# A decoder layer on one core: low parts of the feed-forward weights on GpSimd, and head and last group in a new order

## The reference, cut to what matters

```
x = layernorm(x + gelu(x @ ((w1 @ w2^T) * sparse_mask) + b2))              # x: 4 x 256 x 512
q = x @ wq (32 heads of 128); k, v = ctx @ wk, ctx @ wv (8 groups); rope on q and k
x = layernorm(x + softmax(q k^T / sqrt(128) + mask) v @ wo)                # ctx: 4 x 64 x 512
base = x @ W^T + b
lora = sum over 8 experts of routing[b, e] * (x @ A[e]^T) @ B[e]^T * 2
routing = softmax(mean(x[:, 107:-1]) @ router_W^T + router_b)
out = layernorm(x + base + lora)
```

## Time and profile before

| | |
|---|---|
| median of 3 runs | 487.48 us (487.14 to 487.7) |
| the profiled execution's own time | 488.16 us |
| its span, first to last instruction | 486.4 us |
| TensorE busy | 471.9 us (97%) |
| VectorE busy | 403.4 us (83%) |
| ScalarE busy | 266.2 us (55%) |
| GpSimd busy | 253.8 us (52%) |
| mean granted TensorE clock | 0.990 of full speed |

### The profile page before, as it was taken

How to read it: one execution, slowest core, us unless ns; L and a number is a source line. 1 busy time by engine, 2 the same in 40 slices (tenths; PEclk the granted TensorE clock), 3 DMA queues, 4 the chain that set the end, 5 groups by cost and what they waited for, 6 DMA issues and landing times.

```text
span 486.4 us, 11234 instructions
## 1 busy us (share of the span) xinstructions
PE 471.9 (97%) x4293; PEld 393.0 (81%) x4293; DVE 403.4 (83%) x720; ACT 266.2 (55%) x460; POOL 253.8 (52%) x250
## 2 busy tenths in 40 slices
PE   8999999999999999999999999999999999789994
PEld 7878878887888888888888888888888888568873
DVE  2679988788888887888888888888887999987566
ACT  4573656835483648355644755384637444544434
POOL 3378536954494559356835774486539423022300
PEclk9999999999999999999999999999999999979998
DMA  8945100230023002301320230022002400000004
GB/s 269 355 157 175 44 1 1 89 130 3 1 86 129 0 0 92 123 0 27 112 77 0 84 110 22 0 86 86 0 0 88 67 1 2 1 0 1 0 2 173
DMA packets 29137, 31.56 MB, mean 65 GB/s; under 512 B 6321, under 2 KB 16817, under 8 KB 29114
## 3 DMA queue, kind: packets, MB, share of 16 engines
q1 hardware_dynamic: 29114, 31.25, 20.0%
HBM read 29.15 MB, written 2.10 MB: 64 GB/s over the span
## 4 chain that ended last, share of the span: by engine, by line
PE 94%; DVE 3%; ACT 2%; issue 1%; POOL 0%; POOLq 0%; ACTq 0%; DVEq 0%
PE bank L272 28%; PE bank L274 27%; PE bank L273 27%; PE bank L380 7%; PE bank L278 2%; PE bank L389 2%; DVE VWl L1166 1%; PE bank L293 1%; ACT VWh L813 1%; PE bank L286 0%; DVE QR L1200 0%; PE bank L414 0%; PE bank L447 0%; PE bank L333 0%; DVE X L1425 0%
## 5 line engine op out<-in xcount | busy, mean ns | idle before, releaser
L1760 POOL TENSOR_TENSOR QS<-QS,SIN 128x512 f32<-128x512 f32 x64 | 82.8, 1294 | 118.0 <-ACT QS L813 117.5
L1166 DVE TENSOR_TENSOR VWl<-bank,VWh 64x512 fp32r<-64x512 f32 x128 | 88.0, 687 | 16.0 <-ACT VWh L813 14.4
L272 PE MATMUL bank<-XTh,WQh 128*128 128x512 f32 x256 | 101.0, 395 | 0.0
L274 PE MATMUL bank<-XTh,WQl 128*128 128x512 f32 x256 | 99.8, 390 | 0.0
L273 PE MATMUL bank<-XTl,WQh 128*128 128x512 f32 x256 | 99.8, 390 | 0.0
L813 ACT ACTIVATE VWh<-bank 64x512 fp32r<-64x512 f32 x128 | 76.0, 594 | 29.3 <-PE bank L274 27.1
L813 ACT ACTIVATE QS<-bank 128x512 f32<-128x512 f32 x64 | 38.4, 600 | 70.7 <-PE bank L274 70.4
L272 PEld LDWEIGHTS bank<-XTh,WQh 128*128 128x128 f32 x256 | 48.0, 188 | 10.9 <-issue 0.4
L274 PEld LDWEIGHTS bank<-XTh,WQl 128*128 128x128 f32 x256 | 48.1, 188 | 10.2
L273 PEld LDWEIGHTS bank<-XTl,WQh 128*128 128x128 f32 x256 | 48.1, 188 | 9.8
L1294 DVE TENSOR_TENSOR bank<-bank,COS 128x512 f32<-128x512 f32 x64 | 44.7, 698 | 12.8 <-ACT QS L813 11.6
(11 more groups left out here) (157 smaller groups left out, 936.9 us busy)
## 6 DMA issues: line engine op xcount, KB each, us to landing
WQr<-in_L_xattn_wq_dram SPq DMA_DIRECT2D x8, 1024.0 KB, 5.5
WOr<-in_L_xattn_wo_dram SPq DMA_DIRECT2D x8, 1024.0 KB, 5.5
KVr<-in_L_xattn_wk_dram SPq DMA_DIRECT2D x8, 256.0 KB, 5.0
KVr<-in_L_xattn_wv_dram SPq DMA_DIRECT2D x8, 256.0 KB, 5.3
out_dram<-X SPq DMA_DIRECT2D x8, 256.0 KB, 2.0
X<-in_x_dram SPq DMA_DIRECT2D x3, 512.0 KB, 9.7
WQr<-in_L_attn_w_dram SPq DMA_DIRECT2D x4, 256.0 KB, 4.5
WOr<-in_L_attn_w_dram SPq DMA_DIRECT2D x4, 256.0 KB, 4.8
```

The lines of the kernel that those rows point to most:

```text
L272: pe.matmul(o, lh, rh, start=start, stop=False)
L274: return pe.matmul(o, ll, rh, start=False, stop=stop)
L1166: return dve.tensor_tensor(o, i, f32(hi), ALU.subtract)
L1760: pool.tensor_tensor(q, q, SIN[:, :].unsqueeze(1).broadcast_to([P, 2, S]), ALU.mult)\
```

## The change

Nothing of what is computed changes. Four things do:
- `f_lo(0..5)` moves from DVE to POOL. Since it can't read the bank there, ACT makes a second copy of each transposed weight, `f_raw(j)`, unrounded, into one of the two halves of CTX, and POOL subtracts from that. `f_raw(j)` waits until `f_lo(j - 2)` has read its half. TensorE may reuse the bank when `f_raw` has read it. `f_lo(6)`, a plain copy, stays on DVE.
- The first chunk of the mixing matrix is done in two halves, with `w2_transpose(1)` between, and two of seven warming matmuls go.
- The head's lists are laid anew on all engines: both `ctx_tile` come before `dense(0)`, `x_tile(5)` and `x_tile(6)` later, `x1_tile(0)` before `dense(5)`, `values(0)` before `keys(0)`, and on ACT `wq_hi(0, 0)` before `gelu(0)`.
- The last group and the tail are laid anew on all engines, with other banks; `route_transpose` shares bank 5 with `lora_in(1)`, which now waits for `rt_out`.

The loop over groups 1 to 6 and the DMAs are unchanged.

```diff
-            return (5, 4, 5, 3, 4, 5, 4, 5)[t]
+            return (4, 3, 4, 4, 3, 4, 5, 4)[t]
...
-            return (0, 6, 2, 7, 1, 6, 7, 3)[t]
+            return (7, 1, 2, 3, 6, 1, 3, 0)[t]
...
-        F_BANKS = (1, 2, 1, 0, 2, 1, 3)
-        LORA_BANKS, ROUTE_BANK = (4, 5), 3
+        F_BANKS = (2, 0, 2, 0, 2, 3, 0)
+        LORA_BANKS, ROUTE_BANK = (4, 5), 5
...
             warm(5)
             w2_transpose(0)
-            warm(7)
+            warm(5)
+            attn_chunk(0, 0, 2)
             w2_transpose(1)
-            attn_chunk(0)
+            attn_chunk(0, 2, C)
             w2_transpose(2)
+            w2_transpose(3)
             attn_chunk(1)
...
             pe.wait_ge(sm["tr_lo"], 2)
-            x_tile(5, 5)
+            ctx_tile(0, 5)
             pe.wait_ge(sm["tr_lo"], 3)
-            ctx_tile(0, 6)
+            ctx_tile(1, 6)
+            pe.wait_ge(sm["tr_lo"], 4)
+            x_tile(5, 7)
             pe.wait_ge(sm["at_masked"], 1)
             dense(0)
             pe.wait_ge(sm["at_masked"], 2)
             dense(1)
+            pe.wait_ge(sm["tr_lo"], 5)
+            x_tile(6, 8)
             pe.wait_ge(sm["x_added"], 1)
             dense(2)
...
             x_tile(7, 9)
+            pe.wait_ge(sm["tr_lo"], 9)
+            x1_tile(0, 10)
             pe.wait_ge(sm["x_added"], 4)
             dense(5)
...
             pe.wait_ge(sm["x_added"], n_added(LAST - 1, 7))
-            attend(LAST, 1)
-            pe.wait_ge(sm["x_added"], n_added(LAST - 1, 5))
-            value_out(LAST, 4, 3)
-            pe.wait_ge(sm["x_added"], n_added(LAST, 1))
             value_out(LAST, 5, 6)
-            pe.wait_ge(sm["f_lo"], 1)
-            weight_transpose(2)
             pe.wait_ge(sm["x_added"], n_added(LAST, 0))
             probs_transpose(LAST, 2)
+            pe.wait_ge(sm["vw_lo"], n_vw(LAST, 4))
+            value_out(LAST, 6, 3)
+            pe.wait_ge(sm["q_rot"], n_rot(LAST, 3, 1))
+            weight_transpose(0)
+            pe.wait_ge(sm["q_rot"], n_rot(LAST, 2, 0))
+            weight_transpose(1)
+            pe.wait_ge(sm["vw_lo"], n_vw(LAST, 5))
+            attend(LAST, 1)
+            pe.wait_ge(sm["f_raw"], 1)
+            weight_transpose(2)
             pe.wait_ge(sm["pt_lo"], n_unit(LAST, 2))
             probs_transpose(LAST, 3)
-            pe.wait_ge(sm["vw_lo"], n_vw(LAST, 5))
+            pe.wait_ge(sm["vw_lo"], n_vw(LAST, 6))
+            value_out(LAST, 7, 3)
+            pe.wait_ge(sm["x_added"], n_added(LAST, 1))
             attend(LAST, 2)
+            pe.wait_ge(sm["f_raw"], 2)
+            weight_transpose(3)
+            pe.wait_ge(sm["pt_lo"], n_unit(LAST, 3))
+            attend(LAST, 3)
+            pe.wait_ge(sm["x_added"], n_added(LAST, 2))
+            attend(LAST, 4)
...
             pe.wait_ge(sm["lg_step"], 1)
             route_transpose()
-            pe.wait_ge(sm["tr_lo"], 26)
+            pe.wait_ge(sm["rt_out"], 1)
             lora_in(1)
...
+            def f_raw(j):
+                act.wait_ge(sm["f_mm"], j + 1)
+                if j > 1:
+                    act.wait_ge(sm["f_lo"], j - 1)
+                copy(CTX[:, j % 2, :], bank[:, F_BANKS[j], :]).then_inc(sm["f_raw"], 1)
+
...
+            def f_lo(j):
+                pool.wait_ge(sm["f_hi"], j + 1)
+                pool.wait_ge(sm["f_raw"], j + 1)
+                if j < 4:
+                    m = pool.tensor_tensor(f_part(WQl, j), split2(CTX[:, j % 2, :]), f32(f_part(WQh, j)), ALU.subtract)
+                else:
+                    m = pool.tensor_tensor(WOl[:, j - 4, :], CTX[:, j % 2, :], f32(WOh[:, j - 4, :]), ALU.subtract)
+                m.then_inc(sm["f_lo"], 1)
```

More of the change, by code:

```diff
@@ L310, in attn_part, with attn_chunk @@
                            WQh[:, c, :], WQl[:, c, :], start=c == 0, stop=c == C - 1)
-            def attn_chunk(c):
+            def attn_chunk(c, first=0, end=C):
                 pe.wait_ge(sm["w2t_lo"], c + 1)
@@ L318, in attn_chunk @@
                     pe.wait_ge(sm["w1_lo_rest"], c)
-                for s in range(C):
+                for s in range(first, end):
                     attn_part(c, s)
@@ L738, in _ @@
+            pe.wait_ge(sm["vw_lo"], n_vw(LAST, 7))
+            attend(LAST, 5)
+            pe.wait_ge(sm["f_raw"], 3)
+            weight_transpose(4)
             pe.wait_ge(sm["s_sub"], n_unit(LAST, 3))
             x2_tile(0)
-            pe.wait_ge(sm["vw_lo"], n_vw(LAST, 4))
-            value_out(LAST, 6, 3)
-            pe.wait_ge(sm["q_rot"], n_rot(LAST, 2, 0))
-            weight_transpose(3)
-            pe.wait_ge(sm["x_added"], n_added(LAST, 2))
-            value_out(LAST, 7, 6)
@@ L746, in _ @@
[L746 to L753 removed]
             pe.wait_ge(sm["x_added"], n_added(LAST, 3))
             attend(LAST, 6)
+            pe.wait_ge(sm["x_added"], n_added(LAST, 5))
+            weight_transpose(5)
             pe.wait_ge(sm["x_added"], n_added(LAST, 4))
@@ L757, in _ @@
             attend(LAST, 7)
-            pe.wait_ge(sm["f_lo"], 4)
+            pe.wait_ge(sm["f_raw"], 6)
+            x2_tile(1)
+            pe.wait_ge(sm["x_added"], n_added(LAST, 6))
             base(0)
+            pe.wait_ge(sm["f_raw"], 4)
+            weight_transpose(6)
             pe.wait_ge(sm["tr_lo"], 19)
             x2_tile(2)
-            pe.wait_ge(sm["f_lo"], 2)
-            weight_transpose(4)
-            pe.wait_ge(sm["x_added"], n_added(LAST, 5))
+            pe.wait_ge(sm["q_rot"], n_rot(LAST, 3, 0))
@@ L765, in _ @@
+            base(1)
+            pe.wait_ge(sm["tr_lo"], 21)
             x2_tile(3)
-            pe.wait_ge(sm["x_added"], n_added(LAST, 7))
-            base(1)
             pe.wait_ge(sm["tr_lo"], 20)
             x2_tile(4)
-            pe.wait_ge(sm["f_lo"], 5)
+            pe.wait_ge(sm["f_raw"], 5)
             base(2)
-            pe.wait_ge(sm["tr_lo"], 21)
+            pe.wait_ge(sm["tr_lo"], 22)
             x2_tile(5)
-            pe.wait_ge(sm["f_lo"], 3)
-            weight_transpose(5)
+            pe.wait_ge(sm["s_sub"], n_unit(LAST, 3))
@@ L776, in _ @@
+            x2_tile(6)
             pe.wait_ge(sm["tr_lo"], 23)
-            x2_tile(6)
-            pe.wait_ge(sm["x_added"], n_added(LAST, 6))
             base(3)
@@ L1675, in _ @@
             stats(1, 4)
+            x2_lo(0)
+            accumulate(LAST, 6)
             std_step(1, 1)
-            accumulate(LAST, 6)
             stats(1, 5)
+            x2_lo(1)
+            std_step(1, 2)
             accumulate(LAST, 7)
+            x2_lo(2)
             stats(1, 6)
-            std_step(1, 2)
-            x2_lo(2)
-            f_lo(4)
+            f_lo(6)
             stats(1, 7)
@@ L1698, in _ @@
             out_add(0)
+            stats(2, 0)
+            out_add(1)
             routed_lo(1)
-            out_add(1)
-            stats(2, 0)
             out_add(2)
@@ L1711, in _ @@
             out_add(5)
+            stats(2, 5)
             out_add(6)
-            stats(2, 5)
+            std_step(2, 2)
             stats(2, 6)
-            std_step(2, 2)
             out_add(7)
@@ L1886, in _ @@
             probs(LAST, 3)
+            f_lo(0)
+            f_lo(1)
+            f_lo(2)
+            f_lo(3)
             add_bias(0)
+            f_lo(4)
+            f_lo(5)
             add_bias(1)
```

411 lines of the change are left out of this document (193 added, 218 removed).

## The result

The changed kernel took 486.14 us (median of 10 runs, 485.77 to 487.38), the kernel before, timed with it, 487.73 us (487.14 to 488.43). The ratio is 0.9975, 95% interval 0.9964 to 0.9986: 1.2 us faster by the ratio, 1.6 by the medians. Timed again later beside other kernels it was 0.9980 (0.9969 to 0.9991). The direction is as forecast, the size is less than half of the 3.75 us.

What follows compares the result with a forecast made beforehand. TensorE, busy 97%, loses time waiting for VectorE in the last group. 8.45 - (2.2 + 0.3 + 0.4 + 0.3) = 5.25 us gained, less 1.5 in the head, is 3.75: 487.48 - 3.75 = 483.7 us, range 481.2 to 486.6 (0.8).

Steps and rivals of the forecast that it cites:

- `std_step` beside GpSimd: Last group and tail: `std_step` reads SBUF twice while GpSimd subtracts; 0.3 us lost, bounds zero and 1.3 us per step.
- the clock's 3.4 us: Last group, 420 to 440: TensorE's clock no longer falls, giving back 3.4 us, 1.7 for each of two falls.
- 8.45 us of loss: Last group and tail: the most a new order can give back, 4.8 us waits, 3.4 clock, 0.26 before the fifth base tile.
- The VectorE-bound stretch: Last group, `attend(LAST, 0)` to `attend(LAST, 4)`: TensorE waits 2.2 us in four places; bounds 1.0 and 4.8.
- The route bank: Tail: `route_transpose` shares a bank with `lora_in(1)`, which waits 0.3 us for the copy that frees it.
- The head: Ahead of the loop: 1.0 + 0.3 + 0.6 - 0.4 = 1.5 us lost, 1.0 of it at `dense(2)`; bounds -0.4 and 3.0.
- rival D: Head: a drain of 1.38 us follows the table load before the first gelu; 485.1 us, chance 0.05.
- B: Rival: the head costs nothing, since the gelus catch up; 481.8 us, chance 0.15.
- C: Rival: the last group's new waits still drop the clock once, costing 1.7 us; 485.4 us, chance 0.16.
- E: Rival: VectorE stays the last group's bound, waits shrink only by 2.4 us, clock falls as before; 486.9 us, chance 0.10.
- F: Rival: ring of two CTX halves sets the pace if GpSimd's low parts take over 2.3 us; slower, chance 0.12.
- A: The main forecast: 5.25 us gained in last group and tail, 1.5 lost in the head; 483.7 us, chance 0.42.

Runs made afterwards that it cites:

- e3: The changed kernel with four more waits on GpSimd, so that no GpSimd subtraction or addition lies beside `std_step`; ratio 0.9932 to the kernel before.
- e4: The changed kernel with GpSimd's six `f_lo` and eight `add_bias` cut to 8 columns each, output not the reference's; ratio 0.9932 to the kernel before.
- e2: The kernel before with the new head only, last group and tail as they were; ratio 1.0024 to the kernel before.
- e12: The kernel before with only the six low parts moved to GpSimd, from raw copies by ScalarE, in the old order; ratio 1.0018 to the kernel before.
- e1: The changed kernel with the old head, so new last group and tail only; ratio 0.9943 to the kernel before.
- e5: e3 with the old head; 482.95 us, ratio 0.9901 to the kernel before.
- e7: The changed kernel with the start of the head, up to `dense(0)`, in the old order; ratio 0.9959 to the kernel before.
- e6: e5 with routing logits and `route_transpose` in bank 0 and `out_add(1)` ahead of `stats(2, 0)`; ratio 0.9908 to the kernel before.
- e10: The changed kernel with the six low parts back on VectorE in the new order, without ScalarE's raw copies; ratio 1.0012 to the kernel before.

## Why the prediction was wrong

**The term that failed: `std_step` beside GpSimd, 0.3 us.** It cost 1.9 us (e3 and e4 against after), 1.6 more than I had, and 5.25 - 1.6 = 3.65 is what the traces show of the last group and tail, 3.7. I had the rows for it: one operation at 0.40 us that ended with GpSimd's, a bound of 1.3 us a step, and a count. I took 0.3 since the row with an overlap was short; but its length only said how late in GpSimd's operation it began. The trace of before has a hold of nearly full length too, in its head, which I didn't look for:

```profile
31.78 1.14 DVE L1227 TENSOR_SCALAR RS<-VE 128x2 int32<-128x2 int32 x1
```

It ends at 32.92, and a GpSimd subtraction of 1.30 us that began at 31.60 ends at 32.90. How long a hold is hangs on where the two happen to meet: e2 has the tail of before, instruction for instruction, and instead of the one operation at 0.40 it has two of 1.23 and 1.22 us and a wait of 0.45 on TensorE behind them. And with the change GpSimd would be busy 11.29 us of 20 instead of 3.62, so that a step with four dependent operations of two inputs each would meet it nearly every time. All four steps met it, for 4.0 us on VectorE, of which TensorE paid half.

The Trainium skill (SBUF — State Buffer, "SBUF: two separate sides") has the rule that VectorE's two-input operation and GpSimd's exclude each other, and the five ends of the trace of after agree with it. I had set it aside. That the sum by it, 486.0, meets the measured 486.14 is in part luck: it had two collisions that cost TensorE 2.6 us, and there were five that cost it 1.9.

**The second step: the clock's 3.4 us, and the median.** The 8.45 us of loss came from the one profiled execution of before, with both falls in it (mean clock 0.990), and I took the gain off the median. The 55 executions of before that were timed beside the changed kernels average 0.993. The 15 of them at 0.990 or below took 488.4 us on average, the 20 at 0.995 or above 487.05: 1.3 us apart, where the clock's term was 3.4. In e12 five executions at 0.998 or above took 488.3 us on average, four at 0.990 or below 488.7. So a fall of the clock costs much less than its share of the time in this stretch. A likely reason is that TensorE waits for VectorE there anyway; no run shows it by itself. Of the forecast's miss some 0.4 to 0.7 us is this, the profiled execution of before being that much above its medians (487.73 and 487.48).

**The other terms of the last group.** The VectorE-bound stretch: 0.64 + 0.18 + 0.82 = 1.64 us where I had 2.2. The route bank: 0.26 for 0.3. `x2_tile(6)`: 0.18 for 0.4, once the overlaps are out (e3). The 0.26 us at `base(5)` did not come back: `out_add(1)` was put ahead of `routed_lo(1)` but behind `stats(2, 0)`, which I overlooked; 0.27 is still there. The clock was kept, 1.00 for 0.83. With these the sum without overlaps would be 8.45 - 0.27 - 1.64 - 0.26 - 0.18 = 6.1, and e3 shows 5.6. The other 0.5 is the clock's term again: from B to C TensorE was busy 108.89 us before and 105.97 in e3, 2.9 less and not 3.4. That the rest comes out so well, 3.65 for 3.7, is luck: the stretch that VectorE bounds was 0.56 us too dear, `x2_tile(6)` 0.22, and the clock 0.5 and `base(5)` 0.27 too cheap.

**The head, forecast 1.5 us lost.** The size came out: 1.2 (e2), 1.6 (after against e1), 1.5 (e3 against e5). But some 0.5 of it lies in the loop, for which I had nothing, so that is partly luck, and the places were half right. `dense(2)` did not wait 1.0: `wq_hi(0, 0)` waited for its DMA only until 26.30, not 27.12, the first gelu ran at 28.24, and TensorE came later by itself. In e3, where the DMA landed at 26.98, it waited 0.38, in e4 0.48. So the mechanism is there and its price hangs on the landing. ScalarE's rows of after:

```profile
26.30 0.63 ACT L814 ACTIVATE WQh<-WQr 128x512 fp32r<-128x512 f32 x1 [0.51 <-DMA WQr<-in_L_xattn_wq_dram]
26.95 1.28 ACT L849 ACT_TABLE_LOAD   x1
28.24 0.58 ACT L849 ACTIVATE bank<-bank 128x512 f32<-128x512 f32 x1
```

From table load to gelu are 1.29 us, as before, and the load began right behind the copy; rival D and its drain (the Trainium skill, ScalarE: Activation LUTs, "What ACT_TABLE_LOAD costs") did not show. `x1_tile(0)` waited 0.53 us in after and 0.38 to 0.86 in the seven other traces with the whole new head, for 0.6 forecast, and not at all in e7; `dense(4)` didn't wait. The 0.4 for `ctx_tile(1)` was not there: `dense(0)` began 0.78 us later in after, with `x_lo(1, 1)` ahead of `masked(1)` on VectorE and `x_tile(3)` ahead of the last `attn_last` on TensorE; e7 could not tell this from how the loads land.

**In the loop**, which I had put at nothing, the new head costs some 0.5 us: A to B is 284.03 to 284.07 with the old head (284.32 once, in e6), 284.36 to 284.96 in the eight traces with the new one and 284.12 in e7. What differs lies in the first pass. TensorE has a wait there that nothing which the profile shows as an engine's work ends ("issue"): 0.80 us at 97.54 in after, and 0.64 at 118.11 before; in e7, which has the old start, it is 0.61 us at 118.86.

```profile
97.54 0.50 PE L380 MATMUL bank<-KK,QR 64*64 64x64 f32 x17 [0.80 <-issue]
```

Laid instruction by instruction on before, TensorE in after falls 1.08 us behind at this place and gets 0.59 back at 118, where its wait is gone: that is the whole 0.47, and all later passes are as long as before. The trace also tells what comes just ahead of the wait, wherever it is. The DMA queue that brings instructions (q8) ends a 16 KB transfer at 96.31 in after and at 116.69 in before, and in all fourteen traces TensorE goes on 1.2 to 1.6 us after the end of such a transfer. In the eight traces with the new start, which has four TensorE records fewer ahead of the loop (523 for 527), the wait is near 98, in the six with the old one near 118. So the loop's 0.5 us goes with the new start and most likely with the loading of instructions; no run moved that alone.

**The rivals.** B, a head that costs nothing, fell with e2. C, a fall of the clock in the new order, and E, VectorE as the bound with the clock falling as before, fell with the clock at 1.00. F, the ring of CTX, fell too: no TensorE wait names CTX, and the low parts took 1.28 to 1.30 us. What happened is A with one term mis-sized by 1.6 us, and with a gain that was read off one execution. e12 warns of the same: its trace equals that of before (span 486.3 and 486.4), its ratio is 1.0018.

## What to carry to other kernels

Before moving work to GpSimd, lay its operations beside every short VectorE operation with two inputs in SBUF that someone waits for: each can cost up to the whole of a GpSimd operation, and how likely that is goes with GpSimd's busy share there, not with the one overlap that a trace shows now. A wait on GpSimd for the end of the short steps costs nothing where it has slack, and here it gave 1.9 us. A wait that ends with an engine doesn't say that the engine's load makes it: the same subtractions taken away without the order gained nothing (e12, with GpSimd's holds against it), the order without them 1.4 us, both 3.7. And before a loss that one trace shows is taken off a median, look at how often the executions have it.

## What the runs showed of the hardware

VectorE's short operations were held beside GpSimd's until these ended, as shown above. The hold reaches one-input operations too. In the head of after a `guess` step of 128x2 elements took 0.94 us (33.57 to 34.51) beside a GpSimd subtraction that ended at 34.49, and a `normalize` of 128x512 took 1.60 us, with a GpSimd subtraction begun 0.04 us after it, where the next took 0.69; both read SBUF and write SBUF. Sums with one input in PSUM and the statistics were not held: `accumulate` kept its 0.65 to 0.69 us beside GpSimd.

```profile
33.57 0.94 DVE L1236 TENSOR_SCALAR VE<-MV 128x2 f32<-128x2 f32 x1
38.41 1.60 DVE L1279 TENSOR_SCALAR X<-X,MV,RS 128x512 f32<-128x512 f32 x1 [0.82 <-POOL RS L1751]
40.75 0.69 DVE L1279 TENSOR_SCALAR X<-X,MV,RS 128x512 f32<-128x512 f32 x1
```

The clock. In before TensorE went to half speed (1.2 of 2.4 GHz) after 1.78 and 0.77 us of waiting, and again after 2.00. In e12 it went down once, after the same first two waits (1.77 and 0.77), and stayed down longer (0.50 in the window from 426 to 432). The wait of 0.66 fell into that time; but e2 was down from 426 to 432 too, without a wait there, so that wait is not the reason. The later waits of 1.08 (e12) and 1.44 us (e2) were followed by no fall. In e10 it stayed at 1.00 through 0.64, 0.18, 1.31 and 0.86 us within 12 us, and in after through 1.64 in three pieces.
